# The second load of x moves from SyncE's queue to ACT's, ahead of the activation table load

## The reference

```python
def _layernorm(x, axis=-1, eps=1e-05):
    m = jnp.mean(x, axis=axis, keepdims=True)
    v = jnp.var(x, axis=axis, keepdims=True)
    return (x - m) / jnp.sqrt(v + eps)
...
# block 1: four experts, picked by the token's id; Wg = Wu = Wd = ctx
for e in range(E):
    g = jax.nn.silu(jnp.einsum('bsd,fd->bsf', hidden_states, Wg[e]))
    u = jnp.einsum('bsd,fd->bsf', hidden_states, Wu[e])
    y = jnp.einsum('bsf,df->bsd', g * u, Wd[e])
    out = jnp.where((expert_ids == e)[..., None], y, out)
...
# block 2: router with top 4 of 16 experts of 96 features, and one shared expert
x = x + _L0_xattn_ref(_layernorm(x, axis=-1), ids, ctx_2048, ctx_2048, ctx_2048)
x = x + _L0_ffn_ref(_layernorm(x, axis=-1), ...)
```

## Time and profile before

| | |
|---|---|
| median of 3 runs | 171.93 us (171.66 to 172.04) |
| the profiled execution's own time | 172.95 us |
| its span, first to last instruction | 170.8 us |
| outside the span | 2.15 us |
| PE busy | 164.7 us, 96% of the span |
| DVE, ACT, GpSimd busy | 116.8, 69.1, 37.5 us |

### The profile page before, as it was taken

How to read it: one execution, slowest core, us unless ns; L and a number is a source line. 1 busy time by engine, 2 the same in 40 slices (tenths; PEclk the granted TensorE clock), 3 DMA queues, 4 the chain that set the end, 5 groups by cost and what they waited for, 6 DMA issues and landing times.

```text
span 170.8 us, 2188 instructions
## 1 busy us (share of the span) xinstructions
PE 164.7 (96%) x712; PEld 129.7 (76%) x712; DVE 116.8 (68%) x233; ACT 69.1 (40%) x117; POOL 37.5 (22%) x36
## 2 busy tenths in 40 slices
PE   6899999999999999999999899999999999999992
PEld 2668888888887888887886777887888888788781
DVE  1599599955984988884899685676844444444452
ACT  4640831653258254426370555923512222333320
POOL 2294000295214025570498000000000000000000
PEclk9999999999999999999999999999999999999999
DMA  5999000046402236999112540005372212100003
GB/s 171 307 385 335 6 2 0 0 128 241 123 0 48 96 133 158 276 216 231 36 61 50 165 154 0 4 15 170 102 243 101 64 63 61 61 2 0 4 0 123
DMA packets 11923, 18.50 MB, mean 108 GB/s; under 512 B 3624, under 2 KB 5896, under 8 KB 11784
## 3 DMA queue, kind: packets, MB, share of 16 engines
q1 hardware_dynamic: 11912, 18.36, 35.5%
HBM read 16.13 MB, written 2.23 MB: 108 GB/s over the span
## 4 chain that ended last, share of the span: by engine, by line
PE 72%; DVE 11%; DMA 9%; issue 3%; SPq 2%; ACT 0%; DVEq 0%; POOL 0%; POOLq 0%
PE bank L972 19%; PE bank L1068 10%; PE bank L1066 9%; PE bank L1067 8%; PE bank L1089 5%; PE bank L1086 5%; PE bank L1087 5%; DMA first<-x_d 4%; PE bank L929 3%; DVE prod L806 2%; PE bank L939 2%; DMA x_d<-first 2%; DMA first<-comb_d 2%; DVE xn L680 2%; DMA comb_d<-comb_row 1%
## 5 line engine op out<-in xcount | busy, mean ns | idle before, releaser
L1068 PE MATMUL bank<-xn_lo,gu_hi 128*128 128x512 f32 (+1 forms) x104 | 41.1, 395 | 0.0
L1066 PE MATMUL bank<-xn_hi,gu_lo 128*128 128x512 f32 x96 | 38.0, 396 | 0.9 <-DVE hid L819 0.9
L1067 PE MATMUL bank<-xn_hi,gu_hi 128*128 128x512 f32 x96 | 38.0, 396 | 0.0
L574 ACT ACTIVATE h_hi<-hid 128x512 fp32r<-128x512 f32 (+1 forms) x26 | 16.5, 633 | 50.8 <-DVE hid L819 50.8
L824 DVE TENSOR_TENSOR h_lo<-hid,h_hi 128x512 fp32r<-128x512 f32 (+1 forms) x26 | 19.1, 734 | 14.9 <-ACT h_hi L574 14.9
L1068 PEld LDWEIGHTS bank<-xn_lo,gu_hi 128*128 128x128 f32 (+1 forms) x104 | 19.4, 187 | 4.9
L1066 PEld LDWEIGHTS bank<-xn_hi,gu_lo 128*128 128x128 f32 x96 | 18.0, 188 | 5.6 <-issue 1.3
L708 DVE COPY_PREDICATED prod<-beyond,bank 128x512 f32<-128x512 uint8 x24 | 17.7, 740 | 6.5 <-PE bank L972 5.2
L564 ACT ACTIVATE act_sb<-bank 128x512 f32<-128x512 f32 (+1 forms) x26 | 15.3, 590 | 15.1 <-PE bank L1068 15.0
L1067 PEld LDWEIGHTS bank<-xn_hi,gu_hi 128*128 128x128 f32 x96 | 18.0, 188 | 4.3
L451 POOL TENSOR_TENSOR gu_lo<-stage,gu_hi 128x512 fp32r<-128x512 f32 x12 | 17.2, 1452 | 16.9 <-ACT gu_hi L481 11.5
(11 more groups left out here) (96 smaller groups left out, 219.4 us busy)
## 6 DMA issues: line engine op xcount, KB each, us to landing
stage<-gu_d SPq DMA_DIRECT2D x6, 512.0 KB, 3.8
stage<-wd_d SPq DMA_DIRECT2D x3, 512.0 KB, 4.2
first<-comb_d SPq DMA_DIRECT2D x8, 192.0 KB, 2.7
ids<-comb_d SPq DMA_DIRECT2D x8, 192.0 KB, 3.2
stage<-ctx_d SPq DMA_DIRECT2D x4, 256.0 KB, 5.3
xt<-xt_d SPq DMA_DIRECT2D x1, 1024.0 KB, 9.6
first<-comb_d SPq DMA_DIRECT2D x8, 128.0 KB, 3.1
ids<-comb_d SPq DMA_DIRECT2D x8, 128.0 KB, 2.9
```

Source lines behind the costliest of these rows:

```text
L574: nc.scalar.activation(h_hi[0:w, slot[g]], hid[0:w, g % 2], ACT.Copy).then_inc(hhi_done, 1)
L1066: nc.tensor.matmul(out[:], gu_lo[:, cols], xn_hi[:, h, k], start=(k == 0), stop=False)
L1067: nc.tensor.matmul(out[:], gu_hi[:, cols], xn_hi[:, h, k], start=False, stop=False)
L1068: ins = nc.tensor.matmul(out[0:rows, :], gu_hi[:, wide], xn_lo[:, h, k], start=False, stop=(k == KC - 1))
```

## The change

The transfer of tiles 2 and 3 leaves SP's list, in which it was second, and becomes the first instruction of ACT's list, ahead of the table load. Its source, destination, size and semaphore are the same.

```diff
@@ block.sync
             sp.dma_start(first[:, 0:P + PAIR], first_d).then_inc(x_in[0], 16)
-            sp.dma_start(first[:, P + PAIR:P + 2 * PAIR], x_d[:, 0:PAIR]).then_inc(x_in[1], 16)
             load_piece(0)
@@ block.scalar
+            act.dma_start(first[:, P + PAIR:P + 2 * PAIR], x_d[:, 0:PAIR]).then_inc(x_in[1], 16)
             nc.scalar.preload_act_table(ACT.Silu)
             centre(1)
             centre(3)
```

## The result

The changed kernel takes 172.19 us (median of 22 runs) against 171.31 us for the kernel before (22 runs with it). The ratio is 1.0047, 95% interval 1.0026 to 1.0067: slower by some 0.8 us, where 0.35 to 0.4 was predicted. (A ratio is taken from the single times of both kernels and not from the medians, so the two can differ a little.) The times after stand in two groups, 11 of 22 at 171.30 to 171.78 and 10 at 172.60 to 173.02 (one is at 174.09); those before lie between 170.53 and 172.04 without such a gap, but for two stray ones.

A forecast was written before the change was run, and what follows sets the result against it. PE, busy 96% of the span, was taken as the bound, decided before the first mix. `first_d` 0.42 us late less 0.07 slack gave +0.35; 171.93 + 0.35 = 172.28, say 172.3 us, range 171.7 to 173.2.

The forecast's parts named there:

- Where PE is tight: Before the first mix: `first_d` was said to have only 0.07 us of slack in front of PE.
- the first mix at 8.84: Sign expected on PE after the change: first product of the mix at 8.84 us and not 8.49.
- the clock's step at the same place: Sign expected on PE: its rise from 1.2 to 2.4 GHz stays where the profile before had it, about 7.3 us.
- SP's list moved forward: SP's remaining loads issue 0.45 us earlier; gain on PE's path taken as 0, between 0 and 0.03 us.
- tiles 2 and 3 would land earlier: The moved transfer lands at best 0.46 us earlier, worth nothing, as its readers are busy until 4.70.
- The delay of `first_d`: Start of the kernel: two queues issued together make `first_d` land 0.42 us later, between 0 and 0.65.
- the filling of the slow beginning: From 1.6 to 2.4 us a second queue uses empty room, up to 160 KB, cutting the delay of `first_d` to 0.3.
- my upper bound: `first_d` lands +0.65 us later, near where both transfers end now, if the engines serve both queues in turn.
- whole-packet turns: Engines finish one transfer's share before the other: +0 if SP's came first, +0.58 us after slack if ACT's did.
- PE's clock rises later: Rival: the hole before tile 0 delays PE's clock rise, +1.0 us on top of 0.35, 173.3 us; chance 0.15.
- the slack held: x_d on ACT could land 0.31 us later than today, 4.39 to 4.70, without harm.
- the chance of "slower": Whole kernel: slower was given 0.45, same 0.45, faster 0.10; some 0.34 us can be told from no change.

The follow-up runs named there:

- a hole alone: The kernel before with six instead of eight products of zeroes at PE's start, no transfer touched: 172.18 us, ratio 1.0063.

## Why the prediction was right and wrong

**Where PE is tight: right.** `first_d` was the load with no slack, and the predicted signs came: ACT's issue of 0.39 us, SP's issues from 1.20, a hole on PE in front of tile 0, a late start of tile 0's statistics. Two signs did not come in the changed kernel's profile, the first mix at 8.84 (8.19) and the clock's step at the same place (before 5.8 and not at 7.3). SP's list moved forward brought nothing on PE's path: in the changed profile ACT doesn't even wait for the first weight piece any more, and PE is no earlier for it. That tiles 2 and 3 would land earlier was wrong, they land 0.3 us later; it cost nothing, as DVE was busy with tile 0 until 5.56.

**The delay of `first_d`: right in kind, too small.** I took 0.42 us between 0 and 0.65; this pair of profiles shows 0.87, and the four profiles with 256 KB of x on ACT's queue have DVE starting at 4.38 to 4.62, on average 4.49, against 3.77 for seven without company: 0.72. (The four are the changed kernel and three of the experiments, the seven the kernel before and those in which nothing starts beside `first_d`.) The step that failed is the filling of the slow beginning, by which I came down from 0.65 to 0.42. Two queues did not fill it. The GB/s of the changed kernel, 0 to 8 us in slices of 0.2:
```profile
GB/s 0 0 0 0 0 0 0 0 38 133 64 69 120 200 399 381 402 448 428 354 343 246 256 348 369 379 358 277 266 287 338 318 297 338 359 471 389 440 389 492
```
From 1.6 to 2.4 us 61 KB were moved (38 + 133 + 64 + 69, times 0.2) against 97 before. This single number scatters (61 to 89 KB in the four profiles with two queues, 79 to 143 in the seven without); the time by which 590 KB have been moved is steadier, read off the slices 3.93 to 3.95 us with two queues, against 3.73 to 3.82 in the five that issue both transfers one after the other on SP's queue. So my upper bound, which took the total rate as unchanged, was too low by some 0.15 us, and with it the measured 0.72 fits service in turn.

That the engines took the two transfers in turn can be read from the queues. From 2.8 to 3.2 us and from 3.2 to 3.6 us (packets, MB, share of the engines; q1 is SP's queue, q10 ACT's, and one packet here is one row):
```profile
q1 hardware_dynamic: 33, 0.08, 54.2%
q10 hardware_dynamic: 35, 0.07, 46.1%
...
q1 hardware_dynamic: 36, 0.09, 57.4%
q10 hardware_dynamic: 38, 0.08, 49.9%
```
The two queues go in step. The packets' own times in the trace show it row by row: between 2.4 and 3.9 us, a packet that starts just before another one ends (3 or 4 ns) is of the other queue in 279 cases and of the same queue in 53, where chance would give some 30 of each. And both transfers landed within 0.2 us of each other. This disagrees with both outcomes that I had worked out from the Trainium skill's whole-packet turns ("DMA: Bandwidth & Descriptors", Queues, rings and completion order), +0 and +0.58: neither transfer went first.

**The clock: a part of the result, not a case of its own.** I gave "PE's clock rises later" a chance of 0.15 as something that would happen or not, at +1.35 us over the kernel before. The runs show the middle: about half of the changed kernel's executions are some 1.3 us above the other half, the group vanishes with ten products (ratio 1.0014), and a hole alone costs 1.0063. A hole doesn't decide it by itself: the changed kernel's profile has one of 0.89 us and the high level right behind it. Of seven profiles with a wait of 0.4 us or more in front of tile 0, two had the high level already during the products of zeroes, three have it right behind the wait and two only near 10.6 us; the seven with no such wait have it by 7.3. That the upper group of the changed kernel itself has the late rise was not profiled; it rests on the profile with ACT's issue behind the table load, which is the same start. That profile shows 9.35 to 10.57 us for two products at the low level after a hole of 0.65 us. By the Trainium skill ("TensorE: Matmul & The Clock Gate", Part 1) it is sustained activity that releases the clock; the late rise behind a hole fits this.

**Tiles 2 and 3: the slack held, the landing didn't.** I counted the slack up to the first reader (0.31 us), and no run shows that to be too much: where they landed 2.7 us later, PE waited 2.2. What went wrong, in the expectations of two experiments, is when a transfer lands that isn't first: one place further back in the queue it came 2.7 us later and not 0.5 to 0.9, and issued at 2.10 on ACT's queue it came at 8.4 and not at 5.3.

**The sum.** Late tile and clock together: 0.80 us measured, 0.35 forecast. The sign, the place and the chance of "slower" came from the right term; the number fell short by that term's size and by leaving the clock out of it. That the time itself, 172.19 us, is so near the 172.3 forecast is luck: the forecast stood on 171.93 us for the kernel before, from three runs, and 22 runs give 171.31. This start was 0.6 us too high and the step from it some 0.5 us too small (0.88 by the medians). From one pair of profiles nobody could have seen that the change costs time, since there the changed kernel is 1.5 us shorter.

## What to carry to other kernels

A transfer on which the first compute waits should be alone when it starts. In this kernel another queue was not a free lane: what was issued on it at the same moment was paid for by the critical load, while what stood behind that load in its own queue was not. In a start where PE is kept busy to raise its clock, count a hole at the price of the clock as well as of the wait, and lengthen the filler with the wait. Compare two kernels by many times and look whether they form groups, before reading one profile of each.

## What the runs showed of the hardware that I had not expected

- A DMA issue written behind ACT's table load goes out beside it, at 0.76 us, while the table load runs from 0.73 to 2.01.
- With two queues starting together, fewer bytes moved in the first 0.8 us of data (61 KB against 97 KB in the two profiles), and 590 KB were through 0.1 to 0.2 us later.
- With 128 rows on each, the two queues were served row for row: 33 and 35, 36 and 38 packets in two stretches of 0.4 us.
- An issue on the second queue at 2.10 us, with SP issuing a load every 0.45 us, landed 6.3 us later, against 4.0 when issued at 0.73.
- Two products of zeroes fewer, which leave a hole of 0.90 us in PE's first 7 us, cost 0.9 to 1.1 us over the whole kernel.
